# Regrouping TensorE's work of the last layer, and the ScalarE and VectorE lists with it

## The reference, cut to what matters

```python
X = jnp.fft.rfftn(x, axes=(-2, -1))
Xr, Xi = (jnp.real(X), jnp.imag(X))
Yr = _rconv(Xr, wr) - _rconv(Xi, wi) + b_real[:, None, None]   # 3x3 over frequencies, 16 -> 16 channels
Yi = _rconv(Xr, wi) + _rconv(Xi, wr) + b_imag[:, None, None]
Y = lax.complex(Yr, Yi)
return jnp.fft.irfftn(Y, axes=(-2, -1))
```

## Time and profile before

| | us |
|---|---|
| median of 3 runs | 5653.47 (5628.14 to 5661.97) |
| the profiled execution | 5642.92 |
| its span in the trace | 5641.1 |
| TensorE busy over the span | 5156.6 (91%) |
| VectorE / ScalarE / GpSimd busy | 3344.7 / 2400.4 / 1338.9 |
| granted TensorE clock, mean | 0.985 |

### The profile page before, as it was taken

One profiled execution on the slowest core, in us unless ns is written; L12 is line 12 of the kernel. 1 busy time (PEld: TensorE's weight loads), 2 busy tenths in 40 slices (PEclk: granted clock), 3 DMA queues, 4 the chain that ended last, 5 costly groups with the idle time before them and its releaser, 6 DMA issues. The chain is left out here.

```text
span 5641.1 us, 176368 instructions
## 1 busy us (share of the span) xinstructions
PE 5156.6 (91%) x78733; PEld 2736.3 (49%) x78733; DVE 3344.7 (59%) x5831; ACT 2400.4 (43%) x3042; POOL 1338.9 (24%) x1244
## 2 busy tenths in 40 slices
PE   3999999999999999999999978997775999999999
PEld 3444445444544545554544543344554555555554
DVE  3555555455552443444434437887998677777777
ACT  0222222222221111111111128885997777778776
POOL 0012122122221100000000000003775355555555
PEclk9999999999999999999999989998998999999999
DMA  6889989889977767667667668995887355555554
GB/s 151 211 223 257 262 229 254 256 232 256 261 217 212 196 185 201 180 180 205 178 180 195 183 188 295 321 322 215 310 310 259 92 138 136 135 139 136 138 135 110
DMA packets 330419, 1168.20 MB, mean 207 GB/s; under 512 B 50225, under 2 KB 50977, under 8 KB 278307
## 3 DMA queue, kind: packets, MB, share of 16 engines
q1 hardware_dynamic: 329662, 1156.92, 72.1%
HBM read 683.60 MB, written 455.08 MB: 202 GB/s over the span
## 5 line engine op out<-in xcount | busy, mean ns | idle before, releaser
L625 PE MATMUL c_p<-c_w,wc 128*32 128x512 f16 x55296 | 3042.8, 381 | 152.0 <-issue 115.1
L625 PEld LDWEIGHTS c_p<-c_w,wc 128*32 128x32 f16 x55296 | 1568.3, 97 | 1598.3 <-issue 221.2
L683 ACT ACTIVATE c_t<-c_p,cbias,cscale 128x512 f32<-128x512 f32 x512 | 398.0, 777 | 2645.6 <-PE c_p L625 2645.6
L556 DVE TENSOR_TENSOR a_x<-c_t,a_x 128x512 f32<-128x512 f32 x256 | 175.4, 685 | 906.6 <-ACT c_t L683 900.4
L1610 PE MATMUL f_P<-f_qh,f_wt 64*64 64x512 f16 x4608 | 640.6, 384 | 2.1 <-DVE f_t L1502 2.1
L1610 PE MATMUL f_P<-f_hl,f_wt 64*64 64x512 f16 x4608 | 640.7, 384 | 1.8 <-DVE f_t L1502 1.4
L546 DVE TENSOR_SCALAR c_y<-c_t 128x512 f16<-128x512 f32 x256 | 114.8, 448 | 710.6 <-ACT c_t L683 710.1
L1768 POOL TENSOR_TENSOR f_y<-f_y,f_x 128x512 f32<-128x512 f32 x256 | 330.2, 1290 | 561.5 <-ACT f_y L1742 561.5
L1571 PE MATMUL f_qp<-f_hil,f_gT 128*128 128x260 f16 (+1 forms) x3120 | 439.1, 277 | 3.7 <-DVE f_qh L1486 3.7
L1502 DVE SCALAR_TENSOR_TENSOR f_t<-f_P,f_kk,f_ci 128x256 f32<-128x256 f32 x1024 | 430.4, 476 | 9.0 <-PE f_P L1610 4.4
L1348 POOL TENSOR_TENSOR e_hl<-e_g,e_hl 128x2048 f16<-128x2048 f32 x64 | 261.0, 4079 | 633.1 <-ACT e_hl L1311 633.1
(11 more groups left out here) (250 smaller groups left out, 5974.6 us busy)
## 6 DMA issues: line engine op xcount, KB each, us to landing
c_w<-xs SPq DMA_DIRECT2D x144, 1056.0 KB, 12.2
c_w<-ys SPq DMA_DIRECT2D x144, 1056.0 KB, 11.9
xs<-a_hl SPq DMA_DIRECT2D x72, 1056.0 KB, 9.7
ys<-c_y SPq DMA_DIRECT2D x576, 132.0 KB, 9.7
a_x<-in_x SPq DMA_DIRECT2D x256, 256.0 KB, 9.9
a_x<-in_x SPq DMA_DIRECT2D x128, 512.0 KB, 4.6
x<-a_x SPq DMA_DIRECT2D x256, 256.0 KB, 11.4
d_x<-x SPq DMA_DIRECT2D x64, 1024.0 KB, 8.5
```

Of the source, the lines that this page charges most:

```text
L625: t = p.matmul(pg[32 * j:32 * j + 32, :], wu[:, blk, wl, var, di, :], buf[:, bk, xl * PW + PAD + dx:xl * PW + PAD + dx + NW], start=(di == ...
L683: s.activation(tt_[n % 3][:, :], pp[:, n % 4, :], ACT.Tanh, bias=cbias[:, blk:blk + 1], scale=cscale[:, blk:blk + 1]).then_inc(c_act, 1)
```

## The change

Only the order of steps in the loops changes. TensorE's iteration was round1 (with the row sums), turn, round2, hilbert 0, round3, hilbert 1, correct. It becomes round1, round3, round2, turn, hilbert 0, hilbert 1, correct, and then `begin(i + 1)`: the row sums of the next item, taken out of `round1`. ScalarE's iteration was normal, high, turn, mix, hilbert, correct. It becomes mix, turn, normal, hilbert, high, correct. VectorE's iteration was low, finish, wave(i, 0), wave(i-1, 1), q_low, of which the two waves change places.

```diff
 (VectorE, in the loop over z)
                         low(z + 2)
                     if 0 <= i - 2 < NI:
                         finish(i - 2)
+                    if 0 <= i - 1 < NI:
+                        wave(i - 1, 1)
                     if 0 <= i < NI:
                         wave(i, 0)
-                    if 0 <= i - 1 < NI:
-                        wave(i - 1, 1)
 (TensorE)
-                def round1(i):
+                def begin(i):
 
                     b, ht, n, is_sum = item(i)
-                    if i:
-                        p.wait_ge(f_y0, 2 * i)
-                    if is_sum:
-                        product(i, 0, 0)
-                        return
+                    p.wait_ge(f_y0, 2 * i)
                     if ht == 0:
                         p.wait_ge(se[b], 32)
                     p.matmul(P[:, 0, :], phi[:, ht, :], es[:, b, :], start=True, stop=False)
...
+                def round1(i):
+
+                    if i < NB:
+                        if i:
+                            p.wait_ge(f_y0, 2 * i)
+                        product(i, 0, 0)
+                        return
                     p.wait_ge(f_w1, 2 * i)
...
                         round1(i)
+                    if 0 <= i <= NI:
+                        round3(i)
+                    if 0 <= i < NI:
+                        round2(i)
                     if z < NI:
                         turn(z)
-                    if 0 <= i < NI:
-                        round2(i)
                     if 0 <= z - 1 < NI:
                         hilbert(z - 1, 0)
-                    if 0 <= i <= NI:
-                        round3(i)
-                    if 0 <= z - 1 < NI:
                         hilbert(z - 1, 1)
                     if 0 <= i + 1 < NI and (i + 1) % NB == 0:
                         correct((i + 1) // NB)
+                    if NB <= i + 1 < NI:
+                        begin(i + 1)
 (ScalarE)
                     i = z - LAG
+                    if 0 <= i < NI:
+                        mix(i)
+                    if z < NI:
+                        turn(z)
                     if z + 3 < NI:
                         normal(z + 3)
+                    if 0 <= z - 1 < NI:
+                        hilbert(z - 1)
                     if z + 2 < NI:
                         high(z + 2)
-                    if z < NI:
-                        turn(z)
-                    if 0 <= i < NI:
-                        mix(i)
-                    if 0 <= z - 1 < NI:
-                        hilbert(z - 1)
```

## The result

The changed kernel takes 7037.77 us (median of 4 runs, 7022.23 to 7044.79), the kernel before 5649.17 us in the runs beside it. The ratio is 1.2458, 95% interval 1.2425 to 1.2491: **25% slower**. The forecast was 7110 us with a range of 6650 to 7280.

The account below looks back on a forecast made before the run. TensorE was taken as the bound at 4.74 us an item; a closed loop of 8.83 us plus 1.7 for the clock gave 10.5. Over 248 items +1428, with 29 and 7 on 5643, made 7107, said as 7110; range 6650 to 7280.

Parts of the forecast that it names:

- TensorE's saving: TensorE's iteration: three trips between tilings become one, 0.42 us less, 4.32 us an item; 108 us if TensorE stayed the bound.
- The closed loop: Last layer: from one round1 to the next all steps on three engines lie in a row, 8.83 us an item.
- links 1, 3 and 5: round1(i+1) waits for wave(i,0); low(z+2) for high(z+2); mix(i) for round2(i), hilbert(z-1) for its hilbert 1.
- link 4: ScalarE's high(z+2) now stands last, behind mix(i), turn(z), normal(z+3) and hilbert(z-1).
- link 2: VectorE does wave(i,0) behind low(z+2) in its list, as before.
- second and third term: ScalarE from mix until low starts, 3.71 us; VectorE's low, finish and waves until TensorE starts, 2.92 us.
- The clock: TensorE's wait of 4.6 us in each item lowers its clock: 1.7 us more an item, ends 0 and 2.1.
- The first term: TensorE from the start of round1 to the end of round2, until ScalarE starts: 2.20 us at the full clock.
- rival B: The loop closes but TensorE's clock stays high: 8.83 us an item, 6690 us; chance with its mixtures 0.14.
- The ends: Last layer outside the row items: four sum items +29 us, first six iterations +7, last eight items unchanged.
- With the waves in the old order it would be 0.8 us less: VectorE: without the swap the second wave pair would not lie before TensorE's start, 0.8 us less an item.
- The granted clock of the layer at 0.6 to 0.8: Sign expected in the changed kernel's profile: TensorE's granted clock in the last layer at 0.6 to 0.8.

Follow-up runs that it names:

- e11: The changed kernel with ScalarE's high one item ahead and VectorE's waves in the order of the kernel before: 5532.08 us, ratio 0.9799.
- e13: The kernel before with ScalarE's list mix, turn, normal, hilbert and high one item ahead; TensorE and VectorE as before: 5646.02 us, ratio 1.0012.
- e3: The changed kernel, all orders kept, with ScalarE's high one item further ahead, high(z+3) for high(z+2): 5565.04 us, ratio 0.9842.
- e2: The changed kernel with VectorE's low(z+2) moved from the head of its iteration to the end, behind q_low: 5569.98 us, ratio 0.985.
- e7: The kernel before with ScalarE's changed list alone: 6748.04 us, ratio 1.1961.
- e4: The changed kernel with TensorE's list of the kernel before, ScalarE's and VectorE's lists as changed: 7038.77 us, ratio 1.2476.
- e6: The changed kernel with 20 more TensorE products of 512 columns in begin, their results overwritten: 6678.58 us, ratio 1.1836.
- e5: The changed kernel with VectorE's two waves in the old order, wave(i,0) first: 7028.48 us, ratio 1.2449.
- e8: The changed kernel with ScalarE's high one item ahead and VectorE's low at the end of its iteration: 5566.24 us, ratio 0.9839.

## Why the prediction was right, point by point

**TensorE's saving.** 0.21 us a trip between the tilings, two trips less, 4.32 us an item if TensorE were the bound. e11 has 4.29. It is 111 us under the kernel before of its own set, where 108 was forecast, and e13, without the grouping, is 6 us above that of its set.

**The closed loop.** Its five links stood as given. The waits of the changed kernel show links 1, 3 and 5; e3 (link 4) and e2 (link 2) each open it, e7 shows that ScalarE's list alone closes it, and e4 that it closes without TensorE's grouping. Its size was 8.83 us, term by term 2.20, 3.71 and 2.92. e6, which holds the clock up, has 8.85. The changed kernel itself has 3.70 and 2.92 for the second and third term.

**The clock.** The step "I take 1.7 us" was the term sized worst: it measured 1.4. The first term is 3.62 us, where 2.20 + 1.7 = 3.90 was forecast. The rows it was taken from had the lower level until 3.2 and 4.6 us past the restart; here it is 2.9. That the size came out so near is partly luck. e7's items at the full clock take 8.06 us. By that chain, which I estimate to be e5's as well, e7 loses 1.1 us an item to the clock and e5 2.2; no row of the kernel before could have told which. B's condition is TensorE kept at work, as e6 shows, and B's price of 6690 us came out as 6679. The Trainium skill did not point to rival B as the prediction has it: in "TensorE: Matmul & The Clock Gate", section "Loop structure matters more than you think", the next products follow VectorE's copy immediately. Here TensorE stood idle for 4.5 us, which is another case.

**The ends.** 248 x (10.24 - 4.74) = 1364 us. The last layer is 1385 us longer (1395 less the 10 before it), so sum items, first iterations and drain cost 21 us; 36 was forecast.

**The miss.** The forecast was 72 us too high. The row items are 64 of these (1428 less 1364, the term of the clock), the ends 15, and the rounding up to 7110 another 3; the 10 us before the last layer, which the forecast put at nothing, go the other way.

**Three side remarks failed.** "With the waves in the old order it would be 0.8 us less" holds for the chain (8.06 us in the items of e7 at the full clock) and not for the time: e5 gained nothing, since the lower clock lasted longer. "The granted clock of the layer at 0.6 to 0.8" measured 0.84. And for the kernel as it would be with the loop open I had no chain in mind but TensorE; the one over two items, through `q_low`, cost e3, e2 and e8 0.14 us an item (4.43 for 4.29), and was found only in their traces.

## What to carry to other kernels

Where engines run lists written by hand, follow each wait to the iteration in which it is produced. A step of look-ahead that is moved to the end of its engine's list, while its consumer still puts it first, turns independent iterations into one chain through all engines; the list reads the same and every engine is half idle. Moving the index by one may be the whole repair. When TensorE then waits several us in each turn, price the lower clock too, and do not count on a somewhat shorter chain to give its time back: e5 had none of it back.

Regrouping TensorE's work by tiling was worth some 0.22 us for each trip that went (4.74 to 4.29 for two). It paid 1.6% in e3, and 2.0% (e11) once the buffer that the next group needs first was also freed first on the other engines.

## What the runs showed of the hardware that I had not expected

The time of an item at the oscillating clock did not follow the chain. The changed kernel takes 10.24 us an item at a mean clock of 0.84, and e5, with 0.83 us less on the chain, 10.24 at 0.66. e4, with another TensorE list, takes 10.2 (392 waves in 1000 us) at 0.82, and e7 varies between some 8.06 and 10.35 us around a mean of 9.15. What makes a loop settle at one time or another was not tried.

The clock did not fall at a fixed point of the wait either. In the changed kernel it fell some 4 us after TensorE had stopped, in e5 2.3 us after. In e7 a wait of 3.13 us left it at 1.00 (the restart at 5510.36), and after the next wait it fell when TensorE was at work again, 0.8 us after the restart at 5518.42:

```profile
5518.00:5519.00 1.00, 0.58 (x12) 0.26 (x12) 1.00 (x3) 0.00 (x0) 0.00 (x0) 1.00 0.11 23
5519.00:5520.00 1.00, 1.00 (x16) 0.74 (x8) 0.75 (x2) 0.00 (x0) 0.71 (x1) 0.63 0.61 49
```

More work made the changed kernel faster: 20 products of 512 columns in a wait, whose results nobody reads, took 359 us off by holding the clock at its upper level.
